# Staging q and k for attention: rows in order of dimension, four transfers a group in place of sixteen

## The reference

```python
x = x + 0.5 * ffn(layernorm(x))        # x: (2, 2048, 256)
x = x + attn(layernorm(x))
x = x + 0.5 * ffn(layernorm(x))

# ffn: three products with +-1 weights, 512 -> 1024 -> 1024 -> 256, relu * 2 between
h = s0 * (concat([x, -x]) @ w(k0)); h = relu(h) * 2
h = s1 * (h @ w(k1));               h = relu(h) * 2
h = s2 * (h @ w(k2))

# attn: 16 heads of dimension 16
q, k, v = x @ wq + bq, x @ wk + bk, x @ wv + bv
att = softmax(q @ k.T / 4) @ v
out = att @ wo.T + bo
```

## Time and profile before

| | |
|---|---|
| median of 3 runs | 1593.5 us (1593.01 to 1595.26) |
| the profiled execution | 1593.2 us, its span 1589.4 us |
| PE busy | 1556.4 us, 98% of the span |
| ACT busy | 1066.8 us, 67% |
| DVE busy | 633.1 us, 40% |
| stagings of k | 256 transfers of 128 KB |
| stagings of q | 256 transfers of 32 KB |
| moved in all | 85.04 MB, mean 54 GB/s |

### The profile page before, as it was taken

One profiled execution on the slowest core, in us unless ns is written; L12 is line 12 of the kernel. 1 busy time (PEld: TensorE's weight loads), 2 busy tenths in 40 slices (PEclk: granted clock), 3 DMA queues, 4 the chain that ended last, 5 costly groups with the idle time before them and its releaser, 6 DMA issues.

```text
span 1589.4 us, 29176 instructions
## 1 busy us (share of the span) xinstructions
PE 1556.4 (98%) x11989; PEld 602.1 (38%) x12001; DVE 633.1 (40%) x1414; ACT 1066.8 (67%) x1184; POOL 60.2 (4%) x65
## 2 busy tenths in 40 slices
PE   6999999799999999999999999999999999999999
PEld 3555555223323332333233323323333323323454
DVE  6545664412442244424413343333333333333362
ACT  3222222688788778877877877888788788778621
POOL 2010011000000010010001000000000000000000
PEclk9999999899999999999999999999999999999999
DMA  4010111211211221122111121121211311120010
GB/s 119 27 54 20 35 53 46 74 39 57 71 38 38 72 85 42 41 73 85 40 66 42 50 83 40 53 80 41 77 52 38 91 38 41 52 81 33 27 31 15
DMA packets 57289, 85.04 MB, mean 54 GB/s; under 512 B 7104, under 2 KB 42688, under 8 KB 57152
## 3 DMA queue, kind: packets, MB, share of 16 engines
q1 hardware_dynamic: 56176, 82.60, 15.8%
q10 hardware_dynamic: 976, 0.53, 0.1%
HBM read 61.87 MB, written 21.23 MB: 52 GB/s over the span
## 4 chain that ended last, share of the span: by engine, by line
PE 90%; SPq 4%; DMA 3%; DVE 2%; ACT 1%; issue 1%; ACTq 0%; DVEq 0%
PE psum L757 27%; PE psum L726 21%; PE psum L741 16%; PE psum L629 12%; PE psum L641 7%; PE psum L617 3%; SPq L1062 2%; PE psum L652 2%; PE psum L606 1%; DMA den_t<-den_rows 1%; ACT prob L813 1%; SPq L1060 1%; PE psum L664 1%; DMA q_st<-qk_halves 1%; DVE den_t L952 1%
## 5 line engine op out<-in xcount | busy, mean ns | idle before, releaser
L813 ACT ACTIVATE prob<-psum 128x1024 f32<-128x1024 f32 x1024 | 970.3, 1028 | 245.9 <-PE psum L741 245.9
L757 PE MATMUL psum<-prob,v_sb 128*17 128x512 f32 x4096 | 489.0, 595 | 0.0
L741 PE MATMUL psum<-q_st,k_st 64*128 64x512 f16 x2048 | 346.8, 382 | 12.5 <-DMA q_st<-qk_halves 8.2
L855 DVE TENSOR_SCALAR h_hi<-psum 128x512 f16<-128x512 f32 x140 | 96.1, 686 | 394.6 <-PE psum L726 394.6
L741 PEld LDWEIGHTS psum<-q_st,k_st 64*128 64x128 f16 x2048 | 77.2, 93 | 389.6 <-ACT prob L813 346.0
L789 ACT ACTIVATE h_hi<-psum 128x512 f16<-128x512 f32 x116 | 68.5, 598 | 227.9 <-PE psum L629 166.4
L857 DVE SCALAR_TENSOR_TENSOR h_lo<-psum,h_hi 128x512 f16<-128x512 f32 x256 | 175.6, 691 | 105.3 <-ACT h_hi L789 100.5
L757 PEld LDWEIGHTS psum<-prob,v_sb 128*17 128x17 f32 x4096 | 94.1, 96 | 237.4 <-issue 213.4
L726 PE MATMUL psum<-h_hi,w 64*128 64x512 f16 x1152 | 149.8, 380 | 3.4 <-DVE h_lo L857 2.4
L726 PE MATMUL psum<-h_lo,w 64*128 64x512 f16 x1152 | 147.9, 376 | 0.0
L629 PE MATMUL psum<-h_lo,w 128*128 128x512 f16 x448 | 105.8, 379 | 0.0
(11 more groups left out here) (101 smaller groups left out, 936.4 us busy)
## 6 DMA issues: line engine op xcount, KB each, us to landing
k_st<-qk_halves SPq DMA_DIRECT2D x256, 128.0 KB
qk_halves<-piece SPq DMA_DIRECT2D x32, 256.0 KB, 2.1
q_st<-qk_halves SPq DMA_DIRECT2D x256, 32.0 KB
x_rows<-x_sb SPq DMA_DIRECT2D x16, 256.0 KB, 3.5
att_rows<-o_sb SPq DMA_DIRECT2D x128, 32.0 KB
x_sb<-x_rows SPq DMA_DIRECT2D x8, 512.0 KB, 10.7
att_t<-att_rows SPq DMA_DIRECT2D x16, 256.0 KB
den_t<-den_rows SPq DMA_DIRECT2D x16, 256.0 KB
```

What stands on the lines that cost most here:

```text
L741: mm = pe.matmul(psum[:, 2 * pair + r, :], k_st[rows, slot, t * P:(t + 1) * P], q_st[rows, slot, :], start=True, stop=True)
L757: mm = pe.matmul(psum[32 * j:32 * j + va, O_BANK, :], v_sb[:, b * key_tiles + t, GROUP * g4 + j, :], prob[:, e % PROB_SLOTS, j % 2, :], st ...
L813: act.activation(prob[:, e % PROB_SLOTS], psum[:, 2 * pair:2 * pair + 2, :], ACT.Exp, scale=score_scale / QK_SCALE ** 2).then_inc(exp_sem, 1)
L855: dve.tensor_scalar(hi[:, m, :], psum[:, bank, :], 0.0, None, ALU.max).then_inc(dve_done, 1)
```

## The change

The halves of q and k now go to two DRAM tensors whose rows are in order of dimension. `k_halves` has for each dimension two rows (hi, lo). `q_halves` has for each dimension the pair (hi, lo) twice, so each q piece is stored two times. A pair of heads is then one contiguous run of rows: 128 for q; 64 for k, each read twice in a row. One slot is filled by one transfer for k and one for q, both to all 128 partitions; two slots make four transfers. The order of the 64 rows of a head in SBUF changes with it (by dimension first), the same for k and q, so the product is the same sum. The counts in the semaphore waits follow, q's pieces now counting twice.

```diff
-        qk_dram = internal("qk_halves", (2, 2, dim, tokens), F16)
+        q_dram = internal("q_halves", (dim, 2, 2, tokens), F16)
+        k_dram = internal("k_halves", (dim, 2, tokens), F16)
...
-        STAGE = 16 * 2 * 2 * GROUP
+        STAGE = 16 * 2 * 2
...
+        def pieces_out(m, n):
+
+            return 16 * n * (2 - m % 2)
...
-                        act.wait_ge(piece_out[m], 16 * u)
+                        act.wait_ge(piece_out[m], pieces_out(m, u))
...
-                    dst = qk_dram[m % 2, :, m // 2 * P:(m // 2 + 1) * P, u * BANK:(u + 1) * BANK]
-                    sp.dma_start(dst.rearrange("c p t -> p c t"), piece[:, m]).then_inc(piece_out[m], 16)
+                    dims, columns = slice(m // 2 * P, (m // 2 + 1) * P), slice(u * BANK, (u + 1) * BANK)
+                    if m % 2:
+                        sp.dma_start(k_dram[dims, :, columns], piece[:, m]).then_inc(piece_out[m], 16)
+                    else:
+                        for half in range(2):
+                            sp.dma_start(q_dram[dims, half, :, columns], piece[:, m]).then_inc(piece_out[m], 16)
...
-            for j in range(GROUP):
-                slot, row = g % 2 * 2 + j // 2, 64 * (j % 2)
-                hrows = slice((GROUP * g4 + j) * hd, (GROUP * g4 + j + 1) * hd)
-                for c in range(2):
-                    rows = slice(row + 2 * c * hd, row + 2 * (c + 1) * hd)
-                    sp.dma_start(k_st[rows, slot, :], qk_dram[1, c:c + 1, hrows, keys].broadcast_to((2, hd, seq))
-                                 ).then_inc(staged[g % 2], 16)
-                    sp.dma_start(q_st[rows, slot, :], qk_dram[0, :, hrows, queries]).then_inc(staged[g % 2], 16)
+            for pair in range(2):
+                slot, h = g % 2 * 2 + pair, GROUP * g4 + 2 * pair
+                dims = slice(h * hd, (h + 2) * hd)
+                k_rows = k_dram[dims, :, keys].rearrange("d c t -> (d c) t")
+                sp.dma_start(k_st[:, slot, :], k_rows.unsqueeze(1).broadcast_to((4 * hd, 2, seq))
+                             ).then_inc(staged[g % 2], 16)
+                sp.dma_start(q_st[:, slot, :], q_dram[dims, :, :, queries].rearrange("d k c t -> (d k c) t")
+                             ).then_inc(staged[g % 2], 16)
```

More of the change, by code:

```diff
@@ L799, in act_steps @@
                     if u > redo:
-                        act.wait_ge(piece_out[m], 16 * (blocks + u - redo))
+                        act.wait_ge(piece_out[m], pieces_out(m, blocks) + 16 * (u - redo))
                     else:
-                        act.wait_ge(piece_out[m], 16 * blocks)
+                        act.wait_ge(piece_out[m], pieces_out(m, blocks))
                     bias = (bq_sb, bk_sb)[m % 2][:, m // 2:m // 2 + 1]
@@ L869, in dve_steps @@
                         dve.wait_ge(mm_done, s.mm)
-                        dve.wait_ge(piece_out[m], 16 * u)
+                        dve.wait_ge(piece_out[m], pieces_out(m, u))
                         dve.tensor_scalar(piece[:, m, 0, :], psum[:, bank, :], bias, None, ALU.add).then_inc(dve_done, 1)
@@ L1049, in sp_stage @@
                 for n in range(2 * kd):
-                    sp.wait_ge(piece_out[n], 16 * qblocks * (b + 1))
+                    sp.wait_ge(piece_out[n], pieces_out(n, qblocks * (b + 1)))
             if g >= 2:
@@ L1114, in sp_maxima @@
                     for m in range(2 * kd):
-                        sp.wait_ge(piece_out[m], 16 * 2 * blocks)
+                        sp.wait_ge(piece_out[m], pieces_out(m, blocks) + 16 * blocks)
                     sp.wait_ge(mm_done, done_inputs[0])
@@ L1186, in dve_maxima @@
                     for m in range(2 * kd):
-                        dve.wait_ge(piece_out[m], 16 * 2 * blocks)
+                        dve.wait_ge(piece_out[m], pieces_out(m, blocks) + 16 * blocks)
                 dve.memset(gq[0:1, :], 0.0).then_inc(g_zero, 1)
```

## The result

The changed kernel takes 1582.41 us (median of 4 runs, 1581.50 to 1582.68) against 1594.38 of the kernel before in the same comparison (4 runs, 1593.01 to 1596.88): ratio 0.9922, 95% interval 0.9905 to 0.9939. The forecast was 1582, range 1579 to 1587. The profiled execution took 1582.17 us, its span 1578.2, which is 11.2 less than the span of before.

The account below looks back on a forecast made before the run. TensorE was taken as the bound, busy 1556.4 of 1589.4 us, leaving only idle and low-clock time to win. Start 6.7, clock 2.2 and fetch stalls 2.4 sum to 11.3 us off 1593.2: 1582, range 1579 to 1587.

Parts of the forecast that it names:

- Group 0: Start of attention: four issues end at 263.9, staging lands at 269 to 277, at least 7 us before TensorE is ready.
- What is late next: First score matmul then waits for VectorE's read of PSUM bank 3, starting at 284.30, not 290.97: 6.7 us saved.
- Clock: Behind the remaining 1.5 us gap TensorE keeps full clock, so the sixth scores come sooner: 2.2 us saved.
- Piece stores: Storing each q piece twice moves stage 0's landing by 1 to 2 us, within its cover: no cost.
- Fetches: In attention, denominators fetched behind staging go out sooner and arrive in time; both TensorE stalls for h_lo go: 2.4 us.
- Groups 1 to 31 and the bursts: Later staging is issued a group ahead, and its bursts on all engines don't slow TensorE: nothing directly.
- The sum: Whole kernel: 6.7 + 2.2 + 2.4 = 11.3 us saved from 1593.2, giving 1581.9.
- transfers that don't spread: Rival, 4%: new staging still runs at 47 GB/s, stage 0 lands near 290: 1591 to 1593, about no change.
- The slower rival by strides of HBM: Rival, 3%: HBM serves the new row strides badly, stage 0 lands late; at 40 GB/s 1596.5 us.

Follow-up runs that it names:

- eight-transfer kernel: The changed kernel with eight transfers a group of 64 rows each, on 16 engines, in place of four: 1581.96 us, ratio 0.9927.
- The other banks: The changed kernel with the last two first-layer products of block 5 in PSUM banks 5 to 7, not 2 and 3: 1581.03 us.
- Putting the gap back: The changed kernel with SyncE holding stage 0 back until the last, or the fourth, first-layer product of block 5: 1590.86 and 1587.16 us.
- the rest alone: The changed kernel with both layouts stored, stage 0 by sixteen old transfers, stages 1 to 31 by four new: 1592.92 us, ratio 0.9995.
- the 32-transfer kernel: The kernel before, old layout, with 32 transfers a group of 16 rows each, each copy apart: 1582.39 us, ratio 0.9930.
- The start-alone kernel: The changed kernel with both layouts stored, stage 0 by four new transfers, stages 1 to 31 by sixteen old: 1586.45 us, ratio 0.9954.
- the two-engine kernel: The changed kernel with eight 64-row transfers a group, the two copies as the source's slowest dimension (size 2): 1604.55 us, ratio 1.0064.

## Why the prediction was right, step by step

- Group 0: the landing was estimated at 269 to 277 from 258 and 130 GB/s; the bytes had moved by 268 at 187 GB/s over the stretch, just before the early end. The issues took 2.4 us, 2.6 predicted. The landing is off the path, as argued; the eight-transfer kernel, later by 2.6 us of issues, shows that.
- What is late next: the first score matmul, which waits for VectorE's last read of bank 3, predicted 284.30, measured 284.48 with everything before it 0.2 later. Gap 1.46, predicted 1.5. Counted with that shift the scores start 6.7 us sooner, predicted 6.7. The other banks confirm the cause.
- Clock: 6.42 - 4.26 = 2.2 us, predicted 2.2. Putting the gap back brings the 2.2 back, twice. Two runs had less, 1.8 behind 9.65 us and 1.0 behind 10.97, so the size depends on when the clock returns. That it stays full behind 1.5 us was taken from one wait of 1.56 us, and it held.
- Piece stores: the last k piece is stored at 258.69 and stage 0 issued at 261.43, 2.7 us later, where it was 2.8 to 2.9. Nothing, as predicted. With four more stores a block the rest alone shows that it would have cost where there is no cover (gap 10.97).
- Fetches: out at 889.81, 2.9 us behind the stage's start, 3.3 predicted; both stalls gone, 2.4 us. The transfers are over by 902, over 5 us before VectorE divides at 907.61. The working spoke first of SyncE's queue and did not price by itself that the old fetch also took 15.1 us from its issue to the division; the 32-transfer kernel shows that as the larger part. The start-alone kernel has stalls of 3.2, so 2.4 is the price in the kernel before and need not be that of another.
- Groups 1 to 31 and the bursts: no wait for staging in any of them, exponentials at 1028 ns in both, attention idle time down by 8.1 - 5.7 = 2.4, just the fetch stalls.
- The sum: 11.3 predicted; 6.7 + 2.2 + 2.4 less 0.2 that the part before attention took longer is 11.1, and the profiled times differ by 1593.2 - 1582.2 = 11.0.

Of the rivals, transfers that don't spread did not come here, but the two-engine kernel shows what that would have been: not "about no change" but 22.6 us slower than with 16 engines. My price for it (1591 to 1593) was some 12 us too low: it kept the start as before and the fetch stalls at 2.4 at most, where the gap was 9.65, the stalls 6.9, and the clock low three times. The slower rival by strides of HBM has nothing for it: the new k staging lands in 4.5 us at the median for 512 KB, the stores of q in 2.5. The reason in the change's name, four in place of sixteen, is not the reason of the gain: 32 gain as much.

The Trainium skill ("DMA: Bandwidth & Descriptors", section on why a DMA increments its semaphore by 16) says that a transfer runs on the largest number of engines up to 16 that divides the slowest dimension of both sides. The traces agree: two wherever the source's slowest dimension was 2 (shares 0.13 and 0.12), more wherever it was 16, 32 or 64 (0.32, 0.39, and 0.55 over the 7 us of moving). That it was 16 and not, say, 8 is read from single microseconds only: the changed kernel reached a share of 0.92 from 263 to 264.

## What to carry to other kernels

Before transfers are merged to be fewer, see over how many DMA engines each one spreads: a share that sits at 0.13 while transfers are queued is two engines of sixteen, and a slowest dimension of 2, from a pair of copies or halves, is enough for that. Cutting such a transfer along that dimension can be as good as a new layout. And in an in-order queue look at what stands behind the slow transfers, on an engine with slack: a delay costs nothing until the slack is gone (here 11.9 us), then one for one, and if it stops TensorE long enough (here 2.7 us was, 1.8 was not), the clock on top.

## What the runs showed of the hardware that was not expected

- Issue time on SyncE differs with the transfer's shape, and not in proportion to its rows: 0.42 us for 16 rows, 0.59 to 0.61 for the old 32-row ones with two copies, 0.60 for 64 rows, 0.52 to 0.59 for 128.
- The granted clock fell to 1.2 GHz inside a gap of 4.6 us and cost as much after it (2.2 us) as behind 7.8 and 8.2 us; behind 9.7 us it cost 1.8 and behind 11.0 about 1.0. A longer gap did not mean a higher price.
- The two-engine kernel reached the same low clock a second and a third time, behind waits of 4.1 and 2.7 us for VectorE (6.9 in sum, rounded); granted clock 0.72 and 0.86 over 12 us, a price of 2.7 and 1.7 us. Behind the shorter wait it fell only when TensorE had been at work again for 0.2 us.
